# First stage of a four-layer network kernel: two banks for the up product, one for the gate product, normalisations moved from VectorE to ScalarE, a shorter ranking, and steps of a group dealt out differently

## What is computed

```python
x = x + _L0_xattn_ref(_layernorm(x, axis=-1), ctx_768, ...)   # cosine similarity of projected tokens
x = x + _L0_ffn_ref(_layernorm(x, axis=-1), ...)              # 8 routed experts of 64, top 2, and a shared one of 128
x = x + _L1_xattn_ref(_layernorm(x, axis=-1), ctx_768, ...)   # cross attention, 16 heads
x = x + _L1_ffn_ref(_layernorm(x, axis=-1), ...)              # causal attention, then 8 experts of 256, top 2
```

```python
# _L0_xattn_ref: v, t = two projections to 64 channels
dots = jnp.einsum('bih,bjh->bij', v, t)
denom = jnp.maximum(vn[:, :, None] * tn[:, None, :], EPS)
return dots / denom
# _L0_ffn_ref
sfc = sigmoid(xf @ gate_w) + gate_bias                        # 8 scores for each token
group_scores = top_k(sfc.reshape(T, 4, 2), 2)[0].sum(-1)      # 4 pairs of experts; the best 2 pairs stay
tmp_scores = where(score_mask > 0, sfc, 0); topk_idx = top_k(tmp_scores, 2)[1]
topk_w = topk_w / (topk_w.sum() + 1e-20) * 2.5
g = silu(xf @ w_gate); u = xf @ w_up; experts_y = (g * u) @ w_down
```

## Time and profile before

| | |
|---|---|
| median of three runs | 936.9 us (935.6 to 938.14) |
| the profiled execution | 936.91 us |
| its span in the profile | 934.9 us |
| first stage, up to the last L506 | 0 to about 255.8 us |
| PE busy over the span | 748.2 us (80%) |
| DVE busy over the span | 659.0 us (70%) |
| ACT busy, POOL busy | 394.8 us (42%), 217.2 us (23%) |

### The profile page before, as it was taken

One profiled execution on the slowest core, in us unless ns is written; L12 is line 12 of the kernel. 1 busy time (PEld: TensorE's weight loads), 2 busy tenths in 40 slices (PEclk: granted clock), 3 DMA queues, 4 the chain that ended last, 5 costly groups with the idle time before them and its releaser, 6 DMA issues. The chain is left out here.

```text
span 934.9 us, 26246 instructions
## 1 busy us (share of the span) xinstructions
PE 748.2 (80%) x10100; PEld 554.6 (59%) x10100; DVE 659.0 (70%) x1809; ACT 394.8 (42%) x746; POOL 217.2 (23%) x334
## 2 busy tenths in 40 slices
PE   2579889888728787787888747787774999999998
PEld 1345556555516666665667525565553888888886
DVE  4478878886445888888888657787665666666653
ACT  2122222221122445555555535566542555455553
POOL 4333333331081221133010054244001111111100
PEclk9558888987955999999999958999996999999999
DMA  3000000420113012211220000000000000000000
GB/s 95 20 20 13 18 11 20 124 46 9 16 30 99 29 55 72 73 29 53 75 72 14 13 3 4 4 5 5 4 5 2 1 13 11 11 11 11 11 12 12
DMA packets 33081, 26.41 MB, mean 28 GB/s; under 512 B 9740, under 2 KB 29912, under 8 KB 32984
## 3 DMA queue, kind: packets, MB, share of 16 engines
q1 hardware_dynamic: 29944, 24.07, 9.7%
q10 hardware_dynamic: 3040, 0.98, 0.4%
HBM read 13.51 MB, written 7.34 MB: 22 GB/s over the span
## 5 line engine op out<-in xcount | busy, mean ns | idle before, releaser
L1736 PEld LDWEIGHTS bank<-w2r,hme 128*128 128x128 f32 x1024 | 132.5, 192 | 15.8 <-ACT hme L1590 1.4
L1736 PE MATMUL bank<-w2r,hme 128*128 128x128 f32 x1024 | 135.8, 276 | 0.0
L1590 ACT ACTIVATE hme<-bank,b 128x512 f32<-128x512 f32 x128 | 86.5, 687 | 96.4 <-PE bank L97 96.3
L792 ACT ACTIVATE P<-bank 128x512 f32<-128x512 f32 x128 | 76.6, 598 | 95.4 <-PE bank L985 95.4
L1687 DVE SCALAR_TENSOR_TENSOR Xq<-bank,wgte,Xq 128x128 f32 (+1 forms) x256 | 72.0, 343 | 51.9 <-PE bank L1736 38.4
L915 DVE TENSOR_SCALAR bank<-bank 128x512 f32<-128x512 f32 x128 | 89.0, 695 | 25.0 <-PE bank L976 24.9
L923 DVE TENSOR_REDUCE mx<-bank 128x4 f32<-128x512 f32 x128 | 86.9, 680 | 1.5 <-PE bank L968 1.4
L985 PE MATMUL bank<-mT,negsel 128*128 128x128 f16 x512 | 50.6, 222 | 44.4 <-DVE bank L915 41.7
L350 ACT ACTIVATE sg<-bank 128x512 f32<-128x512 f32 x40 | 23.9, 597 | 127.9 <-PE bank L581 100.2
L985 PEld LDWEIGHTS bank<-mT,negsel 128*128 128x128 f16 x512 | 31.9, 98 | 55.5 <-issue 40.6
L592 PE MATMUL bank<-w_raw,hm 128*128 128x128 f32 x320 | 50.4, 309 | 4.5 <-DVE X L506 4.5
(11 more groups left out here) (372 smaller groups left out, 1740.1 us busy)
## 6 DMA issues: line engine op xcount, KB each, us to landing
cross_q<-qh SPq DMA_DIRECT2D x24, 128.0 KB
K<-cross_k SPq DMA_DIRECT2D x96, 32.0 KB
Q<-cross_q SPq DMA_DIRECT2D x8, 384.0 KB, 3.4
X<-in_x SPq DMA_DIRECT2D x8, 256.0 KB, 2.8
Xq<-X SPq DMA_DIRECT2D x32, 64.0 KB
cross_k<-kh SPq DMA_DIRECT2D x16, 128.0 KB
Yq<-Y SPq DMA_DIRECT2D x32, 64.0 KB
out_x<-Xq SPq DMA_DIRECT2D x32, 64.0 KB, 1.7
```

Source lines behind the costliest of these rows:

```text
L792: act.activation(P[j][:], TB[j % 2][:], ACT.Exp, scale=SCALE).then_inc(s["p_ready"], 1)
L1590: act.activation(hm[:, p % HR], UP[p % RING][:], ACT.Gelu_apprx_tanh, bias=b1[:, p:p + 1]).then_inc(s["gelu"], 1)
L1736: last = pe.matmul(Y[e % 2][:, cols], hm[:, p % HR, cols], w2r[:, p], start=(p % 2 == 0 and i == 0), stop=(p % 2 == 1), skip_group_check=True)
```

## The change

In words, by its parts:

1. **Banks.** The gate product has one bank (GP), the up product two (U0, U1). The gate product waits for Silu of the block before, the up product for `hm` two blocks before.
2. **The routing weight.** Its product into WB is taken out of `up` into `weight(g, p)`, which stands behind `prep(g+2, p)` and `route(g+1, p)` in PE's queue and ahead of `down`. It still waits for `hm` of the block before. `hm` on DVE now waits for it by its own semaphore (`w_psum`).
3. **Normalisation.** Four ACTIVATE instructions with a scale and a bias for each token do on ACT what four TENSOR_SCALAR did on DVE: B in part 0, A in part 3. `root` on POOL has two small operations more (minus the mean, and its product with the root).
4. **Ranking.** One subtraction and one comparison with a mask of tiny thresholds in place of is_gt, is_equal, a product and a sum, for 4 pairs (128 x 64) and for 8 scores (128 x 256).
5. **Order.** `stats("A")` and its `root` move from part 3 to part 1; routing's parts 0, 1, 2 become 1, 2, 3, with the eT transposes still in part 4. The second chain so stands behind `wm`.
6. **No loop.** `sweep` and the loads of SP are written out, without register loops.

```diff
-        P0, P1, PB, G0, G1, UP, WB, DN = bank
-        GP = [G0, G1]
+        P0, P1, PB, GP, U0, U1, WB, DN = bank
+        UP = [U0, U1]
...
-            for g in range(-3, 1):
-                step(g)
-            with eng.Fori(1, G - 3) as g:
-                step(g)
-            for g in range(G - 3, G):
+            for g in range(-3, G):
                 step(g)
...
-                pool.wait_ge(s["eps" + k], g + 1)
-                pool.tensor_tensor(rs[k][:, 1, :], rs[k][:, 0, :], half[:, 0:GB], ALU.pow).then_inc(s["rs" + k], 1)
+                pool.tensor_scalar(rs[k][:, 2, :], mv[k][:, :, 0], -1.0, None, ALU.mult).then_inc(s["eps" + k], 1)
+                pool.wait_ge(s["eps" + k], 3 * g + 2)
+                pool.tensor_tensor(rs[k][:, 1, :], rs[k][:, 0, :], half[:, 0:GB], ALU.pow).then_inc(s["eps" + k], 1)
+                pool.wait_ge(s["eps" + k], 3 * g + 3)
+                pool.tensor_tensor(rs[k][:, 3, :], rs[k][:, 2, :], rs[k][:, 1, :], ALU.mult).then_inc(s["rs" + k], 1)
...
+            def normalise(k, g):
+                act.wait_ge(s["rs" + k], g + 1)
+                for i in range(GB):
+                    last = act.activation(xn[k][:, i, :], xg(g)[:, i, :], ACT.Identity, bias=rs[k][:, 3, i:i + 1],
+                                          scale=rs[k][:, 1, i:i + 1])
+                last.then_inc(s["xn" + k], 1)
...
+                    if p == 0 and has(g + 1):
+                        normalise("B", g + 1)
+                    if p == 3 and has(g + 3):
+                        normalise("A", g + 3)
...
-                    dve.tensor_tensor(room[:, 0], other, own, ALU.is_gt)
-                    link(dve.tensor_tensor(room[:, 1], other, own, ALU.is_equal))
-                    link(dve.tensor_tensor(room[:, 2], room[:, 1], tie, ALU.mult))
-                    link(dve.tensor_tensor(room[:, 1], room[:, 0], room[:, 2], ALU.add))
+                    link(dve.tensor_tensor(room[:, 0], other, own, ALU.subtract))
+                    link(dve.tensor_tensor(room[:, 1], room[:, 0], least, ALU.is_gt))
...
                         dve.wait_ge(s["sg_ready"], k + 1)
-                        after(dve, s["down_psum"], k - NBLK + 1)
+                        dve.wait_ge(s["u_psum"], k + 1)
...
                             dve.wait_ge(s["su_ready"], (NBLK - 1) * g + p + 1)
+                            dve.wait_ge(s["w_psum"], (NBLK - 1) * g + p + 1)
+                            after(dve, s["down_psum"], k - NBLK + 1)
                             dve.tensor_tensor(hm[:, p, :], su[:, i, :], WB[:], ALU.mult).then_inc(s["hm_ready"], 1)
...
             def up(g, p):
                 k = NBLK * g + p
...
-                after(pe, s["sg_ready"], before(k, p) + 1)
-                split_product(pe, GP[i][:], [w[:, 0, p, :] for w in w0], x)
-                after_alone(pe, s["hm_ready"], k, s["carrier"])
-                last = split_product(pe, UP[:], [w[:, 1, p, :] for w in w0], x)
+                after(pe, s["sg_ready"], k)
+                split_product(pe, GP[:], [w[:, 0, p, :] for w in w0], x).then_inc(s["g_psum"], 1)
+                after(pe, s["hm_ready"], k - 1)
+                split_product(pe, UP[k % 2][:], [w[:, 1, p, :] for w in w0], x).then_inc(s["u_psum"], 1)
+
+            def weight(g, p):
+                if p == 0:
+                    pe.wait_ge(s["eT_ready"], g + 1)
                 if p < NBLK - 1:
-                    last = pe.matmul(WB[:], pick[:, p, :], tok(eT, g), start=True, stop=True)
-                last.then_inc(s["gu_psum"], 1)
+                    after(pe, s["hm_ready"], NBLK * g + p)
+                    pe.matmul(WB[:], pick[:, p, :], tok(eT, g), start=True, stop=True).then_inc(s["w_psum"], 1)
...
                     if has(g + 1):
                         route(g + 1, p)
                     if has(g):
+                        weight(g, p)
                         down(g if p >= 2 else g - 1, (p - 2) % NBLK)
```

More of the change, by code:

```diff
@@ L28 @@
 ROUTED_SCALE = 2.5
-GATE_STEPS = 20
+GATE_STEPS = 18
 NBLK = NE * 64 // C + 1
@@ L155, in layer0 @@
         mv = {k: sb("mv" + k, [128, GB, 2]) for k in "AB"}
-        rs = {k: sb("rs" + k, [128, 2, GB]) for k in "AB"}
+        rs = {k: sb("rs" + k, [128, 4, GB]) for k in "AB"}
         half = sb("half", [128, 8])
@@ L186, in layer0 @@
             stB mvB epsB rsB xnB xBT_psum xB_hi xB_lo logit_psum th_ready gate_step carrier wst_ready eT_psum eT_ready
-            gu_psum sg_ready su_ready hm_ready down_psum x2_ready layer1_loaded"""
+            g_psum u_psum w_psum sg_ready su_ready hm_ready down_psum x2_ready layer1_loaded"""
         s = room.sems(names)
@@ L227, in load @@
                 wait_alone(sp, s["c_loaded"], 16 * (g + 1), s["carrier"])
-            over_groups(sp, load, 0, G - 1)
+            for g in range(G):
+                load(g)
             for tile, source in keep["moves"]:
@@ L241, in _ @@
             pool.memset(half[:], -0.5)
-            pool.memset(before4[:], 1.0)
-            pool.memset(before8[:], 1.0).then_inc(s["consts"], 1)
+            pool.memset(before4[:], -2e-38)
+            pool.memset(before8[:], -2e-38).then_inc(s["consts"], 1)
             pool.wait_ge(s["consts"], 1)
@@ L292, in step @@
                         cosines(g + 2, p)
-                    if p == 3 and has(g + 3):
+                    if p == 1 and has(g + 3):
                         root("A", g + 3)
@@ L332, in route @@
             def route(g, part):
-                if part == 0:
+                if part == 1:
                     act.wait_ge(s["xBT_psum"], g + 1)
                     act.activation(tok(xT[0], g), PB[:], ACT.Copy).then_inc(s["xB_hi"], 1)
-                elif part == 1:
+                elif part == 2:
                     act.wait_ge(s["logit_psum"], g + 1)
@@ L347, in step @@
                     if has(g):
-                        act.wait_ge(s["gu_psum"], k + 1)
-                        after(act, s["hm_ready"], before(k, p) + 1)
-                        act.activation(sg[:, p % 2, :], GP[p % 2][:], ACT.Silu).then_inc(s["sg_ready"], 1)
+                        act.wait_ge(s["g_psum"], k + 1)
+                        after(act, s["hm_ready"], k - 1)
+                        act.activation(sg[:, k % 2, :], GP[:], ACT.Silu).then_inc(s["sg_ready"], 1)
                     if has(g + 2):
                         prep(g + 2, p)
+                    if p == 0 and has(g + 1):
+                        normalise("B", g + 1)
+                    if p == 3 and has(g + 3):
+                        normalise("A", g + 3)
                     if has(g + 1):
@@ L379, in stats @@
                 last.then_inc(s["mv" + k], 1)
[L381 to L387, removed]
             steps = 0
@@ L406, in rank @@
                     own = values.unsqueeze(3).broadcast_to(shape)
-                    tie = mask.unsqueeze(1).broadcast_to(shape)
-                    dve.tensor_tensor(room[:, 0], other, own, ALU.is_gt)
-                    link(dve.tensor_tensor(room[:, 1], other, own, ALU.is_equal))
-                    link(dve.tensor_tensor(room[:, 2], room[:, 1], tie, ALU.mult))
-                    link(dve.tensor_tensor(room[:, 1], room[:, 0], room[:, 2], ALU.add))
+                    least = mask.unsqueeze(1).broadcast_to(shape)
+                    link(dve.tensor_tensor(room[:, 0], other, own, ALU.subtract))
+                    link(dve.tensor_tensor(room[:, 1], room[:, 0], least, ALU.is_gt))
                 if part == 0:
@@ L463, in route @@
             def route(g, part):
-                if part == 0:
+                if part == 1:
                     dve.wait_ge(s["xB_hi"], g + 1)
                     dve.tensor_tensor(tok(xT[1], g), PB[:], tok(xT[0], g), ALU.subtract).then_inc(s["xB_lo"], 1)
-                elif part in (1, 2):
-                    gate(g, part - 1)
+                elif part in (2, 3):
+                    gate(g, part - 2)
             def step(g):
@@ L475, in step @@
                     if has(g):
-                        i = p % 2
+                        i = k % 2
                         dve.wait_ge(s["sg_ready"], k + 1)
-                        after(dve, s["down_psum"], k - NBLK + 1)
+                        dve.wait_ge(s["u_psum"], k + 1)
                         if p < NBLK - 1:
-                            dve.tensor_tensor(su[:, i, :], sg[:, i, :], UP[:], ALU.mult).then_inc(s["su_ready"], 1)
+                            dve.tensor_tensor(su[:, i, :], sg[:, i, :], UP[i][:], ALU.mult).then_inc(s["su_ready"], 1)
                             dve.wait_ge(s["su_ready"], (NBLK - 1) * g + p + 1)
+                            dve.wait_ge(s["w_psum"], (NBLK - 1) * g + p + 1)
+                            after(dve, s["down_psum"], k - NBLK + 1)
                             dve.tensor_tensor(hm[:, p, :], su[:, i, :], WB[:], ALU.mult).then_inc(s["hm_ready"], 1)
                         else:
-                            dve.tensor_tensor(hm[:, p, :], sg[:, i, :], UP[:], ALU.mult).then_inc(s["hm_ready"], 1)
```

(17 more changed lines are left out.)

## The result

The changed kernel takes 941.98 us (median of 7 runs) beside 935.6 us of the kernel before: ratio 1.0087, 95% interval 1.006 to 1.0115. The kernel is slower, as forecast, by somewhat less than the 1.1% forecast. The profiled execution has a span of 939.7 us.

What follows compares the result with a forecast made beforehand. A ring through PE's and DVE's queues was to bound the middle groups: 26.0 + 1.1 + 1.7 = 28.8 us against 26.2. Five groups +13.0, the first +3.0, tail -5.9, together +10: 947 us, range 930 to 963.

Steps and rivals of the forecast that it cites:

- The ring: Middle groups: weight product, `hm`, `n2`, `wm`, second chain, eT transposes, next group wait in turn; 26.0 us at full clock.
- the hold: Second chain: POOL's addition to X beside it may hold DVE's comparisons, 0 to 0.8 us, taken as 0.4.
- hand-overs: Around the ring: some eight hand-overs between engines of 0.1 us each, an estimate, 0.8 us together.
- low clock behind the squares: On PE: 6 us at 0.50 follow the sums of squares, slowing two weight products and L548; costs 1.1 us.
- the last two: Tail of the first stage: 16.4 and 13.7 us, together 30.1 where 36.0 were taken, so -5.9 us.
- break-even of 27.1: Middle groups: 27.1 us a group is where the change neither gains nor loses time.
- Rival 3: Middle groups: clock low for most of a group, 30.7 us each, +22 us in all, 959; chance 0.15.
- the weight product's place: On PE: behind `prep` and `route`, with DVE's `hm` waiting for it; named first as what closes the ring.
- The clock on the ring: PE's idle gap ahead of the eT transposes brings 3.4 us at half speed, 1.7 us lost a group.
- Writing the loop out costs nothing: First stage's loop: no idle gap of DVE at a group's start, so 0 counted for the loop's removal.
- ACT's normalisation: On ACT: 1.0 to 1.5 us for each normalisation, lying beside other work.
- The waits of DVE: DVE idles ahead of `hm` in parts 1, 2 and 3 for 1.4, 2 and 2.5 us, ended by the weight product.

Runs made afterwards that it cites:

- after: The changed kernel itself, with all six parts of the change: 941.98 us, ratio 1.0087 to the kernel before.
- e3: Changed kernel with the weight product right behind the up product and the second chain between `su` and `hm` of part 3: 900.68 us, ratio 0.9614.
- e10: The kernel of e4 with the second routing chain moved behind `wm`: 950.64 us, ratio 1.0192.
- e2: Changed kernel with the second routing chain between `su` and `hm` of part 3 instead of behind `wm`: 906.41 us, ratio 0.9693.
- e11: The kernel of e4 with the weight product moved behind `prep` and `route`: 923.65 us, ratio 0.9882.
- e1: Changed kernel with the weight product right behind the up product, ahead of `prep` and `route`: 934.95 us, ratio 1.0019.
- e9: The kernel of e1 with the 18 filling products of e5 ahead of the wait for the second chain: 918.74 us, ratio 0.9831.
- e5: Changed kernel with 18 extra PE products, results overwritten, ahead of the wait for the second chain in groups 1 to 6: 931.86 us, ratio 0.9967.
- e6: Kernel before with only its first-stage register loops written out: 926.13 us, ratio 0.9904.
- e4: Kernel before with one gate bank, two up banks, weight product right behind the up product, own semaphores and no register loops: 920.92 us, ratio 0.9843.
- e7: Kernel before with the short ranking alone: 929.98 us, ratio 0.9957.

## Why the prediction was right, and where it was not

**The ring was there, leg by leg.** From the rows of after above, once round from one eT transpose to the next (144.81 to 172.36), beside the forecast:

| leg | forecast | after |
|---|---|---|
| eT transposes to the end of the sums of squares | 13.2, and 1.7 for the clock | 14.9 |
| logits, weight product, `hm` | 1.4 with `n2` | 1.3 |
| `n2`, `rn`, `dg` | 3.4 | 3.4 |
| L548, weight product | 1.3 | 1.5 |
| `hm`, `wm` | 2.4 | 2.4 |
| second chain | 3.1, and 0.4 for the hold | 3.9 |
| hand-overs | 0.8 | 0.1 left over |
| low clock behind the squares | 1.1 | 0 |
| sum | 28.8 | 27.5 |

**Terms that were mis-sized.** The step "the sums of squares are followed by 6 us at 0.50 ... this costs 1.1" failed in four of the five middle groups of after: in this one PE runs without a gap from 145 to 162 us, and from 149 us on, behind the squares too, the clock is 1.00. Only in the first middle group is it 0.53 behind them (104.6 to 108.0), and that group took 28.1 us, 0.6 more than the next. The first low stretch here (0.52 in 165.7 to 169.0) stands behind the gap of 1.97 us ahead of L548, and what it slows (`down`, block 4) runs beside DVE's work, off the ring: the group before (121.8 to 149.4) has no such stretch, a clock of 0.94 for 0.88, and takes the same 27.5 us. The 0.8 for hand-overs was counted on top of distances between starts that held most of it already. The hold by POOL's addition was 0.95 (1.37 against the 0.42 of e3), more than the 0.8 given as its upper end: the operation whose time was stretched is one with two SBUF inputs that began beside POOL's addition, as the Trainium skill has it (GPSIMD Engine Reference, Specifications), and I should have taken that end. As evidence the forecast named L415 and the operation behind it; L415 has only one input tile, so only the second of them bears on what the page says of two inputs. And beside POOL's power (161.26 to 162.90) the comparisons of the pairs, with two SBUF inputs as well, took 0.23 us, as in the kernel before, so not every operation of POOL holds them. These errors leave 1.3 us too much in a group.

**The sum.** Middle groups +7.1 us (138.2 for 131.1; forecast 13.0), the first one +4.0 (29.5 for 25.5; forecast 3.0), the start +1.0 (forecast 0), the last two -6.0 (30.0 for 36.0; forecast -5.9, by two errors that cancel: 17.1 and 12.9 us for 16.4 and 13.7). Together the stage is 6.2 us longer; the span only 4.8, as the later stages, whose code is the same, took 1.4 less in this profile. Between the profiled kernels that part differed by up to 6 us (673 to 679), so a few us of any single span are not the edit's. A middle group grew by 1.4 us where 2.6 were forecast, and at 27.6 us it lies 0.5 above the forecast's own break-even of 27.1: the way it went was right by a small margin, and the total came as near as it did because the start and the first group cost 2 us more than forecast. Rival 3 didn't show: the clock was 0.87 to 0.94 in the middle groups. The forecast shows no working for its 30.7 us.

**What closed the ring.** The forecast named the weight product's place first. The runs give the order: the second chain behind `wm` is the cause (e10 imposes it: +3.5%; e2 undoes it: -3.9%), the weight product a small part (e11: +0.4%, not clear of noise; e1: -0.7%), of 1.0 to 1.4% with the gap filled (e9 against e5). In e11 the chains still stand where DVE would wait.

**The clock on the ring** was right in mechanism, shown by e5: 18 useless products ahead of the wait make the kernel 1.2% faster. The forecast of 1.7 us a group for it stands beside 1.1 measured over the five middle groups, in spite of the filling's own delay.

**"Writing the loop out costs nothing" was the wrong step,** though it didn't move the forecast, since the ring was set against the traced group of before with its loop in it. I looked for a gap at the loop's turn, and DVE shows none at 88.67, 113.96, 141.73 or 167.59. That says little of the page that the forecast drew on: the Trainium skill (Runtime: NRT & Kernel Launch, Instruction fetch mechanics) names a stall only for a branch to a target outside what has been fetched, and no row here shows whether these targets were. A part of the cost stands inside the group, ahead of waits on a register's value. DVE's timeline of before, in the loop:

```profile
162.51 0.38 DVE L378 BATCH_NORM_AGGREGATE mvA<-stA 128x2 f32<-128x6 f32 x4 [0.15 <-DVE stA L374]
```

The same operation in e6, and the second normalisation:

```profile
158.10 0.38 DVE L375 BATCH_NORM_AGGREGATE mvA<-stA 128x2 f32<-128x6 f32 x4
...
161.67 1.12 DVE L382 TENSOR_SCALAR xnB<-X,mvB,rsB 128x128 f32<-128x128 f32 x4 [0.42 <-POOL rsB L266]
```

The wait ahead of the aggregation is 0.15 us before and not marked in e6; the wait for POOL's root is 0.76 and 0.42 in e6. In the group from 192.87, the first behind the loop, both kernels wait 1.43. (The loop's form of such a wait, `wait_alone`, also adds a semaphore increment; e6 takes out both.) e6's groups take 24.2 to 25.6 us, three of six 24.5; those of before 25.3 to 27.8, and their low stretches are longer (0.88 on average over four groups, 0.93 in e6). Side by side, the waits are the smaller part. The loop's first group takes 25.29 us before and 24.54 in e6, both at a clock of 0.93: 0.75 us, which is about what the marked waits add up to (0.34 and two of 0.15). Its last one takes 25.28 and 25.43, with the same clocks. So the waits are worth 0 to 3 us over the loop's four groups, an estimate from these two pairs, of the 7.5 us by which the stage is shorter. The rest stands where the clock of before was lower: 27.8 for 24.5 us (0.82 for 0.93), 25.9 for 24.5 (0.87 for 0.93), and 26.9 for 24.2 (0.81 for 0.93) in the group behind the loop, whose code is written out in both. Why the clock stayed up in e6 is open, so the 1.0% is shown for the edit and not for the waits. So the change hid a gain of 1.0% (loops) and about 0.6% (banks, e4 against e6) under a loss by its order of parts. More lay under it: e3, with the rest of the change in place and the chain moved, stands 2.3% below e4. Of that rest only the short ranking was tried alone (e7, -0.4%).

**Small terms.** ACT's normalisation took 1.64 us for four, above my 1.0 to 1.5; the Trainium skill (ScalarE: Activation LUTs, What ACT_TABLE_LOAD costs) gives about 280 ns and 0.833 ns for each element with a pointer operand, and some 93 ns for each further one, less as much where they overlap. By that, 0.39 each is an estimate, and the trace's 0.41 agrees. It was hidden, as forecast. The waits of DVE were forecast as 1.4, 2 and 2.5 us in parts 1 to 3 and are 1.30, 1.93 and 2.27; the last group takes 12.9 us, forecast 13.7.

## What to carry to other kernels

When an engine's queue is the bound, its sum says what relief is worth only until some ring through several queues is longer: before moving work within a hand-written schedule, go once round from a product to the same product of the next group, through every in-order queue, and add up. Where an in-order engine must wait for another, put work there that nobody downstream waits for behind it; here 3 us of ranking moved by a few lines, from behind the waiting operation to ahead of it, were worth 3.9% of the kernel, more than all the work taken off DVE. And judge a bundle by its parts: this one held several gains and one loss.

## What the runs showed that I had not expected

- Writing out the loops of this stage gained 1.0% (e6), without any gap at the loop's turn on DVE. Waits on register values account for at most some 3 us of the stage's 7.5, by estimate; the rest came with a higher clock, even in a group that no loop covers.
- The clock didn't follow from the last gap alone. In one group of after, gaps on PE of 2.0 and 2.7 us were each followed by 3.3 to 3.4 us at 0.52, and 13.4 us of unbroken work with the sums of squares in it (149.0 to 162.4) stayed at 1.00. But in the group before it the same gap of 1.97 us was followed by 4 us at 1.00, and in the first middle group a low stretch began behind the squares with no gap since the transposes, 16 us earlier (the three lines below). In the kernel before the low stretch behind the squares came with a gap of only 0.4 us near it. What decides is open.
- One addition of 1.37 us on POOL stretched one DVE operation from 0.42 to 1.37 us, in each of the five middle groups, and left the one ahead of it, begun earlier, at 0.42.

```profile
136.94 1.13 PE L548 MATMUL bank<-dg,ones 128*128 128x512 f32 x2 [1.97 <-POOL dg L282]
...
104.60:108.00 3.40, 3.40 (x20) 2.52 (x18) 2.27 (x10) 0.20 (x1) 1.73 (x2) 0.53 0.00 0
137.00:141.00 4.00, 3.47 (x17) 1.89 (x17) 2.59 (x7) 0.60 (x1) 0.09 (x1) 1.00 0.02 4
```
